# A decoder layer on one core: sums of squares ahead of the output projection, inputs turned between the two parts of the down projection

## What is computed

```python
# step 1: gated linear recurrence
i, f, g = x @ Wi.T, x @ Wf.T, x @ Wg.T
a = sigmoid(f);  h = scan(a, silu(i) * (1 - a))          # along the tokens
xg = h * silu(g)
y = xg * rsqrt(mean(xg**2) + EPS) * w_norm               # the mean square
x = layernorm(x + y @ Wo.T)                              # output projection
# step 2: wkv, a recurrence over the tokens with x as key, ctx as value
x = layernorm(x + wkv(w, u, x, ctx))
# step 3: gated MLP on int8-like rounded rows (x, both weights, hidden)
gate, up = split(q(x) @ q(w_gate_up).T)                  # 2 x 1408 columns
x = layernorm(x + q(silu(gate) * up) @ q(w_down).T)      # down projection
```

## Time and profile before

| | us |
|---|---|
| median of 3 runs | 435.67 (434.51 to 436.34) |
| the profiled execution | 435.61 |
| its span in the trace | 433.8 |
| PE busy | 386.3 |
| DVE busy | 364.1 |
| ACT busy | 320.3 |
| POOL busy | 217.1 |
| mean granted clock of TensorE | 0.977 of full |

### The profile page before, as it was taken

One profiled execution on the slowest core, in us unless ns is written; L12 is line 12 of the kernel. 1 busy time (PEld: TensorE's weight loads), 2 busy tenths in 40 slices (PEclk: granted clock), 3 DMA queues, 4 the chain that ended last, 5 costly groups with the idle time before them and its releaser, 6 DMA issues.

```text
span 433.8 us, 8164 instructions
## 1 busy us (share of the span) xinstructions
PE 386.3 (89%) x2906; PEld 305.5 (70%) x2906; DVE 364.1 (84%) x620; ACT 320.3 (74%) x422; POOL 217.1 (50%) x266
## 2 busy tenths in 40 slices
PE   7898989989898899989998999899989998577873
PEld 7797889877876597759774977597758776333431
DVE  3879698493998799989898998899888989899684
ACT  3668678639926799589957996699759884986671
POOL 1554465243542865457435942594258436626451
PEclk9899999989999999999999999999999999888998
DMA  7946350663020002030203020302030202000101
GB/s 261 351 165 244 115 214 20 232 50 91 2 98 1 2 0 75 2 122 2 73 2 122 3 74 0 121 0 73 0 121 0 73 0 73 2 25 2 48 13 62
DMA packets 12843, 31.75 MB, mean 73 GB/s; under 512 B 2038, under 2 KB 5132, under 8 KB 12812
## 3 DMA queue, kind: packets, MB, share of 16 engines
q1 hardware_dynamic: 12812, 31.35, 21.8%
HBM read 27.14 MB, written 4.21 MB: 72 GB/s over the span
## 4 chain that ended last, share of the span: by engine, by line
PE 43%; ACT 18%; DVE 15%; issue 12%; POOL 5%; DMA 3%; SPq 1%; ACTq 0%; POOLq 0%; DVEq 0%
PE proj_ps L476 24%; PE slot_ps L579 10%; PE slot_ps L612 3%; PE turn_ps L510 2%; POOL ring L1257 2%; ACT xqT L920 2%; DVE ring L1585 2%; ACT L978 2%; ACT hqT L943 2%; DMA ring<-w_gate_up_dram 2%; DMA ring<-w_down_dram 2%; DVE ring L1588 2%; ACT turn_ps L883 2%; ACT L982 1%; DVE xg_low L1451 1%
## 5 line engine op out<-in xcount | busy, mean ns | idle before, releaser
L579 PE MATMUL slot_ps<-w1q,xqT 128*128 128x512 bf16 (+1 forms) x384 | 83.1, 367 | 10.5 <-ACT xqT L920 7.6
L1257 POOL TENSOR_TENSOR ring<-ring 128x512 f32<-128x512 f32 (+1 forms) x48 | 60.5, 1263 | 33.6 <-ACT ring L929 33.6
L579 PEld LDWEIGHTS slot_ps<-w1q,xqT 128*128 128x128 bf16 x384 | 36.8, 99 | 48.8 <-issue 7.9
L476 PE MATMUL proj_ps<-x_high,proj_high 128*128 128x256 f32 x384 | 65.8, 294 | 2.1 <-DVE inp L1465 2.0
L476 PE MATMUL proj_ps<-x_high,proj_low 128*128 128x256 f32 x384 | 62.5, 285 | 0.0
L476 PE MATMUL proj_ps<-x_low,proj_high 128*128 128x256 f32 x384 | 62.4, 284 | 0.0
L476 PEld LDWEIGHTS proj_ps<-x_high,proj_high 128*128 128x128 f32 x384 | 54.2, 192 | 3.9 <-issue 2.4
L476 PEld LDWEIGHTS proj_ps<-x_high,proj_low 128*128 128x128 f32 x384 | 53.9, 193 | 0.0
L476 PEld LDWEIGHTS proj_ps<-x_low,proj_high 128*128 128x128 f32 x384 | 53.4, 191 | 0.0
L929 ACT ACTIVATE ring<-ring,zero_bias,x_scale 128x512 f32<-128x512 f32 (+1 forms) x48 | 36.9, 774 | 12.3 <-DVE ring L1585 11.8
L612 PE MATMUL slot_ps<-w2q,hqT 128*128 128x512 bf16 x176 | 42.1, 388 | 4.3 <-ACT hqT L943 3.3
(11 more groups left out here) (133 smaller groups left out, 845.7 us busy)
## 6 DMA issues: line engine op xcount, KB each, us to landing
ring<-w_gate_up_dram SPq DMA_DIRECT2D x11, 512.0 KB, 5.0
forget<-xT_dram SPq DMA_DIRECT2D x8, 512.0 KB, 3.9
x_sb<-x_dram SPq DMA_DIRECT2D x8, 512.0 KB, 3.7
c_sb<-cT_dram SPq DMA_DIRECT2D x8, 512.0 KB, 4.1
out_dram<-z SPq DMA_DIRECT2D x16, 256.0 KB, 2.0
ring<-w_down_dram SPq DMA_DIRECT2D x4, 704.0 KB, 5.7
scale_rows<-scratch_dram SPq DMA_DIRECT2D x2, 704.0 KB, 5.9
x<-wfT_dram SPq DMA_DIRECT2D x2, 512.0 KB, 5.6
```

The source lines that it names most:

```text
L476: last = nc.tensor.matmul(out, a, b, start=(i == 0), stop=(i == len(terms) - 1))
L579: last = nc.tensor.matmul(slot_ps[:, s, half * 512:half * 512 + width], xqT[:, par, d, t * P:(t + 1) * P], w1q[:, d, half * I + at:half * ...
L1257: nc.gpsimd.tensor_tensor(hid, hid, gate_buf[:, at:at + width], ALU.mult).then_inc(hid_ready, 1)
```

## The change

In iteration(), sum_squares(b+2) is issued ahead of both blocks of project_out(b+2) instead of between them. mlp_down takes an argument, parts, and issues only those parts; iteration() issues part 0 of block 0's down projection, then turn_inputs(b+1), then part 1. The head and the tail keep their order. No instruction is added or removed.

```diff
-            def mlp_down(n, t):
+            def mlp_down(n, t, parts=(0, 1)):
 
                 s = (t + NC) % 2
-                pe.wait_ge(mlp_read, chunks_read(n))
-                for part, (first, count) in enumerate(PARTS):
+                if parts[0] == 0:
+                    pe.wait_ge(mlp_read, chunks_read(n))
+                for part in parts:
+                    first, count = PARTS[part]
                     pe.wait_ge(hq_ready, 2 * n + part + 1)
                     for i in range(first, first + count):
                         last = nc.tensor.matmul(slot_ps[:, s, 0:D], hqT[:, i, :], w2q[:, i, :],
                                                 start=(i == 0), stop=(i == IB - 1))
-                last.then_inc(down_done, 1)
+                if parts[-1] == 1:
+                    last.then_inc(down_done, 1)
...
                 turn_hidden(n, 0, 0)
                 turn_hidden(n, 0, 1)
+                sum_squares(b + 2)
                 project_out(b + 2, 0)
-                sum_squares(b + 2)
                 project_out(b + 2, 1)
-                mlp_down(n, 0)
+                mlp_down(n, 0, (0,))
                 turn_inputs(b + 1)
+                mlp_down(n, 0, (1,))
```

## The result

The changed kernel takes **447.93 us** (median of four executions, the lowest 444.33) against 435.28 before. The ratio is 1.0252, with a 95% interval of 1.0216 to 1.0287; it leaves out the slowest execution, 452.18 us, which lies more than 1.5% above the fastest and has no trace. So it is slower, as forecast in sign, but by 12.7 us instead of 2.7, and outside the range of 436.0 to 442.5.

The account below looks back on a forecast made before the run. PE, busy 89% of the span, was taken as the bound, so only its idle time could be won. Four periods of +0.50 us and a tail of +0.72 took 435.61 to 438.3 us; the 8-in-10 range was 436.0 to 442.5.

Parts of the forecast that it names:

- Step 1: Ahead of the output projection PE waits 1.77 us for z2_ready instead of xg_low, starting 1.14 us later; earlier sums gain nothing.
- Step 2: Ahead of mlp_up, the moved down-projection matmuls cover ACT's copy and give back 1.08 us; mlp_up starts 0.06 us later.
- Step 3: At the next first projection PE waits 0.44 us for POOL's x_low and starts 0.50 us later, four times.
- Rival 2: x_low's chain has more slack than read: no change, 435.9 us, or about 437 with half the slack; chance 0.15.
- rival 3: At the output projection, sum_squares starts no later than the projection did before: faster, 432.6 us; chance 0.06.
- The tail: After iteration 5, turn_keys needs x1 and starts 0.72 us later, and the tail hangs on it.
- rival 1: Behind the new stall the clock falls, 1.7 us each; one to three falls give 440.0 to 443.4 us; chance 0.32.

Follow-up runs that it names:

- the run with transposes: Changed kernel with 28 identity transposes put into PE's new stall ahead of sum_squares, no data wait changed: 441.70 us.
- the stall apart from the sums: Changed kernel with project_out(0), sum_squares, project_out(1) in the old order behind a bare wait for z2_ready: 440.29 us.
- the doubled sums: Kernel before, order unchanged, with every sum of squares computed twice in place, no new wait: 453.64 us.

## Why the prediction was wrong, point by point

**Step 1 was right.** PE stands still 1.74 us ahead of sum_squares (forecast 1.77), and the wait for xg_low is gone. The earlier sums won nothing, as worked out: DVE takes them at 227.07. One reading was loose: of the five waits for xg_low in the earlier trace rows the first, 0.47 us, lies in the head at 38.51, and in iteration 1 the gap ahead of the output projection was 0.42 us, put to no engine, not 0.64. There the new stall is 1.67 us.

**Step 2 was right.** The wait for the copy is 0.20 us, and the split alone doesn't cost. What the step called hidden with 0.3 us to spare had less: DVE has read the first chunk at 239.03 (238.35 + 0.68), and PE's third chunk starts at 239.12. Two slips in that sum changed nothing: 233.37 + 4.33 is 237.70 and not 237.67, and the three small operations end 2.31 us behind 232.62 (234.72 + 0.21 = 234.93), not 2.23.

**Step 3 was right.** x_low ends at 238.15 + 2.36 = 240.51, which is 8.73 us behind the second residual_1 at 231.78, the same 8.73 as in the rows before, and PE starts 0.23 us later, 5.96 behind mlp_up's start instead of 5.50. The last row of PE shows only 0.16 of that as idle, since the end of the matmuls ahead is modelled. A period without a fall was 45.43, forecast 45.46. Rival 2 and rival 3 are refuted by that, and the two runs with an earlier x_low show it from the other side: without the split nothing is won, and the split on top wins 3.7 us on the same chip (434.81 to 431.15).

**The tail** was forecast at +0.72, which is 0.66 behind the copy. turn_keys did start later by that: 3.54 us behind the copy instead of 2.90, so 0.64. The tail grew by 2.2 us, though. 34.8 us behind the copy 24 matmuls of mlp_up, hit by a fall, took 6.62 us where the trace before has 4.93. Whether that is the rest isn't shown: in the run with dense work in the stall the same 24 take 4.93 us and the tail is 68.8 us all the same, with a fall 53 us behind the copy. No run here controls where the tail's falls land.

**The step that failed is the weighing of rival 1.** The forecast of 438.3 us put the clock at nothing. The mechanism was named, and its price per fall of 1.7 us came close to the 1.54 measured. Its chance, 0.32, and its number, one to three falls, were wrong: there were seven. Against periods of 45.43 the six in the four periods cost 9.3 us, and the one in iteration 1 another 1.5 (48.30 against 46.80 in the run with transposes, which had no fall there): 10.8 us. The waits made 2.0 us up to the last copy, of which 1.8 in the four periods. That is the 12.8 us between the two profiled executions, since the tail's +2.2 and the head's -2.2 cancel, by luck.

I compared the new stall of 1.77 us with other stalls only, found it nearer to the harmless one of 1.69, and took the 1.7 us of sum_squares behind it as work. Two things were missed. The run with the stall apart from the sums shows that a bare stall of this size isn't harmless: one fall in five iterations. In iterations 3 and 5 of the changed kernel, too, the fall begins before the one-column matmuls have done more than 0.17 us, so the stall was enough to start it, and they only stood in the time at the low clock. And the doubled sums show that one-column matmuls with no stall next to them bring falls in five of five. By the table both count alike, and the change had put them end to end. I had even written that sum_squares "now stands right behind it", and gave that no weight in the chance.

The rule that I cited from the Trainium skill ("TensorE: Matmul & The Clock Gate", section "Part 1: The HAM clock gate"), that the gate follows its own schedule, agrees with the runs in its consequence: kernels with middling stretches fell in one, two or four of five otherwise equal iterations, the low clock began at different places of the same code, and executions of one kernel differed by up to 6.3 us (435.02 to 441.31 in the run with dense work and an earlier x_low).

## What to carry to other kernels

When an order is changed, look at what now stands next to each stall on TensorE: a wait of 1.7 us, which with full products behind it brought the clock down in one of five iterations, did so in every iteration with thin matmuls of one column behind it, and 12.7 us were lost where the waits alone explain 2.7. Keep thin work on TensorE apart from stalls and in small pieces between dense products. And before a saving on one path is booked, follow the next chain to its end: the split's 1.08 us per iteration were worth nothing until x_low was made earlier, and then 0.93 to 1.04 of it came through.

## What the runs showed of the hardware

TensorE's granted clock fell to 1.2 GHz while the profile shows the engine busy without a pause: in the run with doubled sums, all of 221 to 232 us holds one wait of 0.64 us, and the clock still fell at 232.6, behind 3.5 us of fp32 matmuls with one moving column. A busy share of 1.00 on PE doesn't say that the clock will stay up; what the matmuls stream does matter. With the second half of that time, 1.7 us, spent on 512-column bf16 matmuls instead, the clock stayed at 1.00.
